# VectorE and SP zero stack rows, images and joined weights moved, sum of projections begun ahead, finer steps and a new merge table in a two-layer transformer kernel

## What is computed

```
h  = softmax over the batch of (cond . x) / sqrt(128), times x
x1 = x + bitlinear(silu(bitlinear(h, w_gate)) * bitlinear(h, w_up), w_down)
        # weights ternary, activations rounded to 8 bit per row; inner width 512
c  = causal attention, 16 heads of 8, over x1 plus one image key and value per head
        (k_img, v_img from cond), then c_proj
m  = attention, 16 heads of 8, no mask, over c (in_proj), then out_proj
x3 = layernorm(c + m) * g1 + b1
moe: router over 4 groups x 2 experts; out = weight * (relu(x3 W1 + b1) W2 + b2),
        8 experts of width 256, all computed for all rows
y  = x1 + layernorm(x3 + moe) * g2 + b2
```

## Time and profile before

| what | value |
| --- | --- |
| median of 3 runs | 382.31 us (380.33 to 384.16) |
| profiled execution, time | 381.2 us |
| profiled execution, span | 379.4 us |
| VectorE busy | 261.2 us (69%) |
| ScalarE busy | 171.2 us (45%) |
| GpSimd busy | 42.5 us (11%) |
| mean granted TensorE clock | 0.927 of full |

### The profile page before, as it was taken

How to read it: one execution, slowest core, us unless ns; L and a number is a source line. 1 busy time by engine, 2 the same in 40 slices (tenths; PEclk the granted TensorE clock), 3 DMA queues, 4 the chain that set the end, 5 groups by cost and what they waited for, 6 DMA issues and landing times.

```text
span 379.4 us, 5450 instructions
## 1 busy us (share of the span) xinstructions
PE 307.3 (81%) x1900; PEld 153.9 (41%) x1900; DVE 261.2 (69%) x763; ACT 171.2 (45%) x246; POOL 42.5 (11%) x56
## 2 busy tenths in 40 slices
PE   0251985897898999868999989999999987987980
PEld 0120733253453644433433222343434455655760
DVE  3979457997786887869989878877721135557444
ACT  2664134005455657443678565665777511220210
POOL 9189500000000000000000000002000001001001
PEclk9996566558999999999999999999999999999997
DMA  6101307601670004710006700160000000000001
GB/s 184 46 2 18 46 0 214 146 1 50 177 141 1 3 4 148 184 41 2 2 14 189 168 4 0 29 196 2 2 2 0 0 2 0 3 0 28 2 0 29
DMA packets 14719, 19.69 MB, mean 52 GB/s; under 512 B 2142, under 2 KB 12258, under 8 KB 14116
## 3 DMA queue, kind: packets, MB, share of 16 engines
q1 hardware_dynamic: 14404, 19.06, 19.3%
q0 software_dynamic: 288, 0.28, 0.6%
HBM read 13.99 MB, written 4.72 MB: 49 GB/s over the span
## 4 chain that ended last, share of the span: by engine, by line
PE 48%; DVE 24%; issue 14%; DMA 6%; ACT 5%; POOL 1%; SPq 1%; POOLq 0%; DVEq 0%; ACTq 0%
PE ps_pv L1273 11%; DVE mx L972 8%; PE ps_s L1232 8%; PE ps_t L1255 7%; DMA Qs<-nmT 5%; PE ps_s L1342 4%; PE ps_misc L1350 3%; PE ps_misc L1208 2%; DVE shared L968 1%; DVE shared L809 1%; DVE probs L902 1%; DMA X<-in_x 1%; ACT probs L751 1%; PE ps_misc L1238 1%; DVE mx L968 1%
## 5 line engine op out<-in xcount | busy, mean ns | idle before, releaser
L751 ACT ACTIVATE probs<-ps_t 128x1024 f32<-128x1024 f32 (+2 forms) x128 | 106.6, 862 | 62.9 <-PE ps_t L1258 33.9
L972 DVE TENSOR_REDUCE mx<-ps_s 128x1 f32<-128x512 f32 x128 | 82.0, 686 | 14.2 <-PE ps_s L1232 14.0
L1232 PE MATMUL ps_s<-Ks,Qs 128*128 128x512 bf16 (+3 forms) x237 | 78.0, 353 | 9.5 <-DVE mx L972 3.0
L1255 PE MATMUL ps_t<-Qs,Ks 128*128 128x512 bf16 (+3 forms) x256 | 67.9, 340 | 5.2 <-DMA Qs<-nmT 5.1
L1273 PE MATMUL ps_pv<-probs,Vs 128*32 128x512 f32 (+3 forms) x512 | 57.2, 524 | 0.4 <-ACT probs L751 0.2
L968 DVE CUSTOM_DVE_ANT_0 shared<-ps_s,shared 128x256 bf16<-128x256 f32 (+3 forms) x109 | 47.3, 465 | 10.9 <-PE ps_s L1232 10.3
L1232 PEld LDWEIGHTS ps_s<-Ks,Qs 128*128 128x128 bf16 x237 | 22.4, 99 | 65.5 <-DVE mx L972 30.8
L1074 DVE SCALAR_TENSOR_TENSOR shared<-ps_misc,comb,shared 128x128 f32<-128x128 f32 x64 | 18.1, 344 | 31.3 <-PE ps_misc L1350 31.1
L1350 PE MATMUL ps_misc<-Ks,shared 128*128 128x128 f32 x256 | 31.6, 277 | 5.5 <-DVE shared L1074 2.4
L1255 PEld LDWEIGHTS ps_t<-Qs,Ks 128*128 128x128 bf16 x256 | 23.5, 98 | 30.9 <-issue 8.0
L1350 PEld LDWEIGHTS ps_misc<-Ks,shared 128*128 128x128 f32 x256 | 30.5, 192 | 11.9 <-issue 11.5
(11 more groups left out here) (240 smaller groups left out, 361.9 us busy)
## 6 DMA issues: line engine op xcount, KB each, us to landing
parts_q<-Qp SPq DMA_DIRECT2D x20, 128.0 KB, 2.0
Qs<-parts_q SPq DMA_DIRECT2D x24, 96.0 KB
Ks<-parts_k SPq DMA_DIRECT2D x24, 96.0 KB
Qs<-parts_q SPq DMA_DIRECT2D x12, 192.0 KB
Ks<-parts_k SPq DMA_DIRECT2D x12, 192.0 KB
parts_k<-Kp SPq DMA_DIRECT2D x12, 128.0 KB, 1.8
Ks<-in_L_ffn_w SPq DMA_DIRECT2D x1, 1024.0 KB, 5.8
X<-in_x SPq DMA_DIRECT2D x2, 256.0 KB, 4.4
```

Source lines behind the costliest of these rows:

```text
L751: act.activation(probs[:, half % 2, j, 0:w], ps[:, 0:w], ACT.Exp).then_inc(free[f"t{i % 2}"], 1)
L972: last = dve.tensor_reduce(mx[:, b, t, h:h + 1], ps[:, 0:w], AX, ALU.max)
L1232: mm = pe.matmul(ps[:, 0:w], Qs[:, b, h, t * P:(t + 1) * P], Ks[:, b, h, 0:w], start=True, stop=True)
L1255: mm = pe.matmul(ps[:, col:col + w], Ks[:, b, h, kb * P:(kb + 1) * P], Qs[:, b, h, S - w:S], start=True, stop=(a >= 2))
```

## The change

- **Zeroing.** GpSimd no longer zeroes the upper stack rows. VectorE zeroes those of Qs, batch 0, as its first instruction; SP copies them to the three other stacks by DMA behind the loads of `setup`. A new step `fixed_rows` (SP) writes the constant rows and waits for these copies; so does the send of instances 0 and 1. The value stacks stay on GpSimd, each zeroed in four instructions.
- **Start.** Rounding of batch 1 is a step `round_x` of its own, behind `turn_down`. The image values and joined weights are a step `images` of their own. The residual of a batch is a step `x1` of its own (VectorE), apart from the transposes `x1t`.
- **Sum.** TensorE begins the sum in `presum` (one bias matmul over 512 columns, then the first projection) and ends it in `sum`. The sum of batch 1 lies in bank pv instead of misc. X3, the norm statistics and the router's transposed weights have a place for each batch.
- **Finer steps.** Engine parts that stood in one step have steps of their own: q_parts, k_parts, send, v_bias (VectorE, VectorE, SP, VectorE); image (TensorE); keep (ScalarE); normalise, centre, spread, routed, acc0, add (VectorE); relu (ScalarE and VectorE). centre has also the power on GpSimd, spread the second half of the norm. GpSimd's small loads are a step `load_small` that comes in the attention of instance 3.
- **Merge table.** The table is new, with 681 steps for 576. Spelled out, it begins: setup, ffn_in 0, turn_down, round_x, ffn_up 0.0, ffn_in 1, ffn_up 0.1 to 0.3, turn_weights, ffn_up 1.0, r2t and down 0.0 to 0.3, prepare, x1 0, ffn_up 1.1, images, ffn_up 1.2, x1t 0, ffn_up 1.3, q 0, k 0, q_parts 0, k_parts 0, r2t and down 1.0 to 1.3, x1 1, stacks 0, fixed_rows, send 0, stacks 1, scores 0.0 to 0.28, x1t 1, scores to 0.35, max 0.0, image 0.0, scores to 0.39, q 1, scores to 0.42, max_rows 0.0, scores to 0.45, k 1, scores to 0.48, v 0, q_parts 1, scores 0.49, attend 0.0. The old one has ffn_up 1.0 to 1.2 ahead of the first r2t, prepare with the images ahead of x1t 0, x1t 1 ahead of scores 0.0, then scores to 0.37, max 0.0, scores to 0.41, v 0, scores to 0.45, q 1, max_rows 0.0, scores to 0.47, k 1, scores to 0.49, attend 0.0. After the last values the new one goes: hidden 0.2, normalise, turn_back, hidden 0.3, o_rows, relu, presum 1, add, y 0.2, relu, sum 1, hidden 0.4, y 0.3, centre 1, hidden 0.5, add, relu, spread 1, y 0.4, add, hidden 0.6, x3t 1, y 0.5, hidden 0.7, router 1, ..., and ends hidden 1.7, y 1.6, add, centre, spread, out, y 1.7.

The diff, cut to its core:

```diff
+SUM_AT = ("misc", "pv")
 MERGE = (
-...
+    "ffwTfgfffwgffffffffwugUgfgff44ggggggggvSV4S00000000000000000000000000000g0000000mi0000g000m000g0"
+    "00f50A0AAE0A050Ag0AA500FAA00a00i000a1a1mM1aA1Am1A111a11A1A1A1A11aaI11AA1M1aa1A1A11a11IAA1a1A1A1A"
...
+    "C3m3lC3C3c33c3C3cD33cDK33cO3D3DcK3D3dSD33c3DD33n33QQnddDdPD3D3dLD33Dn3D3DmnDQmdQexddDdPDnDeDnDDd"
+    "QDLxddDDyzDLDPddDzDdDdDDyPxdddeLdedxszyxseyRezxRyzesyesxzxRRzyesxyzxesyRozexyoezxzyeyxezxyzexyey"
+    "zxzzpoppy"
...
+        "w": [("turn_down", 0, 0), ("turn_weights", 0, 0), ("prepare", 0, 0)],
+        "S": [("stacks", 0, 0), ("stacks", 1, 0), ("load_small", 0, 0)],
+        "T": [("round_x", 0, 0)],
+        "U": [("images", 0, 0)],
+        "V": [("fixed_rows", 0, 0)],
         "g": ffn(1) + qkv(1),
+        "u": [("x1", 0, 0)],
+        "v": [("x1", 1, 0)],
+        "i": both("image", 2),
         "m": [(n, a, g) for a in range(INST) for g in range(2) for n in ("max", "max_rows")],
         "q": qkv(2),
         "r": qkv(3),
         "l": [("load_experts", 0, 0)],
-        "n": route(0),
-        "s": route(1),
-        "e": each("hidden", 0, EXPERTS) + each("hidden", 1, EXPERTS),
-        "y": each("y", 0, EXPERTS) + each("y", 1, EXPERTS),
-        "o": [("out", 0, 0)],
-        "p": [("out", 1, 0)],
+        "e": both("hidden", EXPERTS),
+        "x": both("relu", EXPERTS),
+        "y": both("y", EXPERTS),
+        "z": both("add", EXPERTS),
     }
     for a in range(INST):
         chains["0123"[a]] = each("scores", a, HEADS * NT)
+        chains["4567"[a]] = [(n, a, 0) for n in ("q_parts", "k_parts", "send")]
+        chains["EFGH"[a]] = [("v_bias", a, 0)]
         chains["ABCD"[a]] = each("attend", a, UNITS)
         chains["abcd"[a]] = output(a)
+        chains["MNOP"[a]] = each("keep", a, ROUNDS)
+        chains["IJKL"[a]] = each("normalise", a, ROUNDS)
+    for b in range(B):
+        chains["ns"[b]] = [(n, b, 0) for n in ("presum", "sum", "x3t", "router", "combine", "bias2")]
+        chains["QR"[b]] = [(n, b, 0) for n in ("centre", "spread", "routed", "route", "acc0")]
+        chains["op"[b]] = [("centre", b, 1), ("spread", b, 1), ("out", b, 0)]
...
+                    sp.wait_ge(rows_first, 1)
+                    for stack in (Ks[HALF_ROWS:, 0, :, :], Qs[HALF_ROWS:, 1, :, :], Ks[HALF_ROWS:, 1, :, :]):
+                        sp.dma_start(stack, Qs[HALF_ROWS:, 0, :, :]).then_inc(rows_zeroed, 16)
+                if step == "fixed_rows":
                     sp.wait_ge(pool_const, 1)
                     sp.wait_ge(mparts_ready, 1)
+                    sp.wait_ge(rows_zeroed, 16 * 3)
...
-                if step == "v":
+                if step == "send":
                     if a >= 2:
                         sp.wait_ge(free["misc"], filled("misc", "o_rows", b))
                         sp.dma_start(Qs[SHIFT:MASK + PARTS, b, :, :],
                                      zrow[:, :].unsqueeze(1).to_broadcast([2 + PARTS, HEADS, S]))\
                           .then_inc(no_extra[a], 16)
+                    if a < 2:
+                        sp.wait_ge(rows_zeroed, 16 * 3)
...
-                    then_wait(pool.memset(Qs[HALF_ROWS:, 0, :, :].rearrange("p h s -> p (h s)").bitcast(fp32), 0.0))
-                    pool.memset(Ks[HALF_ROWS:, 0, :, :].rearrange("p h s -> p (h s)").bitcast(fp32), 0.0)\
-                        .then_inc(rows_zeroed[0], 1)
-                    pool.wait_ge(rows_zeroed[0], 1)
                 if step == "stacks":
-                    then_wait(pool.memset(Vs[:, 0, :, :, :], 0.0))
-                    pool.memset(Vs[:, 0, :, :, HD:HD + 1], 1.0).then_inc(stack_init[0], 1)
-                    pool.wait_ge(stack_init[0], 1)
-                    then_wait(pool.memset(Qs[HALF_ROWS:, 1, :, :].rearrange("p h s -> p (h s)").bitcast(fp32), 0.0))
-                    pool.memset(Ks[HALF_ROWS:, 1, :, :].rearrange("p h s -> p (h s)").bitcast(fp32), 0.0)\
-                        .then_inc(rows_zeroed[1], 1)
-                    pool.wait_ge(rows_zeroed[1], 1)
-                    then_wait(pool.memset(Vs[:, 1, :, :, :], 0.0))
-                    pool.memset(Vs[:, 1, :, :, HD:HD + 1], 1.0).then_inc(stack_init[1], 1)
+                    for t in range(NT):
+                        last = pool.memset(Vs[:, a, t, :, :], 0.0)
+                    then_wait(last)
+                    pool.memset(Vs[:, a, :, :, HD:HD + 1], 1.0).then_inc(stack_init[a], 1)
+                if step == "load_small":
                     for dst, src in (
...
-                if step in ("sum", "out"):
-                    norms += 1
-                    pool.wait_ge(ve_ready, norms)
-                    pool.tensor_tensor(rstd[:, :], ve[:, :], halves[:, :], ALU.pow).then_inc(rstd_ready, 1)
+                if step == "centre":
+                    n = 2 * i + a
+                    pool.wait_ge(ve_ready[n], 1)
+                    pool.tensor_tensor(rstd[:, n, :], ve[:, n, :], halves[:, :], ALU.pow).then_inc(rstd_ready[n], 1)
...
-                    ps = take("pv", "values", a, i // NT)
-                    act.activation(Ou[:, i // NT % 2, :], ps[:, :], ACT.Copy).then_inc(free["pv"], 1)
-                if step == "hidden":
+                if step == "keep":
+                    ps = take("pv", "values", a, i)
+                    act.activation(Ou[:, i % 2, :], ps[:, :], ACT.Copy).then_inc(free["pv"], 1)
+                if step == "relu":
                     ps = take("s1", "hidden", a, i)
...
+            def centre(n, src, dst, gain):
                 for t in range(NT):
-                    last = dve.bn_stats(stats[:, t, :], src[:, t, :])
+                    last = dve.bn_stats(stats[:, n, t, :], src[:, t, :])
                 then_wait(last)
                 for t in range(NT):
-                    last = dve.bn_aggr(mv[:, t, :], stats[:, t, :])
+                    last = dve.bn_aggr(mv[:, n, t, :], stats[:, n, t, :])
                 then_wait(last)
-                norms[0] += 1
-                dve.tensor_scalar(ve[:, :], mv[:, :, 1], EPS, None, ALU.add).then_inc(ve_ready, 1)
-            def norm(src, dst, gain, more, read_out, count):
+                dve.tensor_scalar(ve[:, n, :], mv[:, n, :, 1], EPS, None, ALU.add).then_inc(ve_ready[n], 1)
                 for t in range(NT):
-                    read = dve.scalar_tensor_tensor(out=dst[:, t, :], in0=src[:, t, :], scalar=mv[:, t, 0:1],
+                    read = dve.scalar_tensor_tensor(out=dst[:, t, :], in0=src[:, t, :], scalar=mv[:, n, t, 0:1],
                                                     in1=norm_gb[:, gain, :], op0=ALU.subtract, op1=ALU.mult)
-                read.then_inc(read_out, 1)
-                dve.wait_ge(read_out, count)
-                dve.wait_ge(rstd_ready, norms[0])
+                return read
+            def spread(n, dst, more):
+                dve.wait_ge(rstd_ready[n], 1)
                 for t in range(NT):
-                    last = dve.scalar_tensor_tensor(out=dst[:, t, :], in0=dst[:, t, :], scalar=rstd[:, t:t + 1],
+                    last = dve.scalar_tensor_tensor(out=dst[:, t, :], in0=dst[:, t, :], scalar=rstd[:, n, t:t + 1],
                                                     in1=more(t), op0=ALU.mult, op1=ALU.add)
                 return last
...
                 if step == "setup":
+                    dve.memset(Qs[HALF_ROWS:, 0, :, :].rearrange("p h s -> p (h s)").bitcast(fp32), 0.0)\
+                       .then_inc(rows_first, 1)
...
                     ternary(0)
+                    ternary(1)
                     rounded_x(0)
-                    ternary(1)
                     then_wait(dve.tensor_scalar(q1[:, 2, :], q1[:, 0, :], 1.0 / 127.0, None, ALU.mult))
                     dve.tensor_scalar(q1[:, 4, :], q1[:, 2, :], wmean[:, 1:2], None, ALU.mult)
                     dve.tensor_scalar(q1[:, 3, :], q1[:, 2, :], wmean[:, 0:1], None, ALU.mult).then_inc(scale_ready, 1)
+                if step == "round_x":
                     rounded_x(1)
...
+                if step == "centre" and i == 0:
                     dve.wait_ge(in_moe, 16 * 9)
-                    norm_stats(take("misc", "sum", a)[:, :].rearrange("p (t d) -> p t d", d=D))
-                    norm(place["misc"][:, :].rearrange("p (t d) -> p t d", d=D), X3[:, :, :], 0,
-                         lambda t: norm_gb[:, 1, :], free["misc"], filled("misc", "sum", a)).then_inc(x3_ready, 1)
-                if step == "router":
+                    ps = take(SUM_AT[a], "sum", a)[:, :].rearrange("p (t d) -> p t d", d=D)
+                    centre(a, ps, X3[:, a, :, :], 0).then_inc(free[SUM_AT[a]], 1)
...
+                if step == "presum":
+                    pe.wait_ge(bias_ready, 1)
+                    pe.wait_ge(free["misc"], filled("misc", "o_rows", a))
+                    ps = put(SUM_AT[a], "sum", a)
+                    pe.matmul(ps[:, :].rearrange("p (t d) -> p t d", d=D), ones[0:1, :],
```

(21 more changed lines are left out.)

119 lines of the change are left out of this document (61 added, 58 removed).

## The result

The changed kernel took **354.04 us** in the median of 4 runs (352.93 to 355.0), the kernel before 381.32 beside it (380.18 to 384.16): ratio 0.927, interval 0.921 to 0.934. That is 27.3 us less; I had forecast 15.2 less, 366 us, with a range down to 356. The sign was right and the size was not. The profiled execution took 352.93 us, its span 351.1 where the one before had 379.4.

The account below looks back on a forecast made before the run. TensorE, busy in 81% of the span, was taken as the bound from the first attention weights to the last values. Gains 7.5 + 1.5 + 0 + 0.8 + 5.4 = 15.2 us, from 381.2 us, gave 366 us, range 356 to 375.

Parts of the forecast that it names:

- Start, 7.5: Everything up to the first scores: 7.5 us faster, bounds 4 to 11.
- (a): Start: the four big memsets leave GpSimd, so VectorE's stalled L824 gives 1.25 us and L913 3.1 us.
- (e): Start: the old L919 stall, 1.3 us, goes; the Vs memsets left on GpSimd cost the new L919 0.9 (0 to 1.8).
- (f): Start: images and joined weights moved behind batch 0's residual and one up step; 1.3 us given back, x1t 6.7 earlier.
- rival 1: TensorE's clock comes back early, speeding images, q, k and the first scores: 5 to 7 us better, 360; chance 0.2.
- First scores, 1.5: First scores to first attend: VectorE's wait for q's first part goes, TensorE becomes the bound; 1.5 us faster, -1 to 2.7.
- Middle, 0 and 0.8: Attention to last values: order gives 0 us (minus 5 to plus 5), merging the first sum's four bias matmuls 0.8.
- Tail, 5.4: Last values to last y: fewer TensorE waits, second bias and layout give 5.4 us, bounds 2.5 to 7.
- The layout: Tail: new step order laid out, ending 62.9 us after the last values against 68.3.
- End, 0: Norm and store after TensorE's last matmul: the last 8.8 us are the same chain, no gain.

Follow-up runs that it names:

- first stage in the old order: Changed kernel with the steps from the first scores to attend step 3 in the order of the kernel before: ratio 0.945 to the kernel before.
- steps coupled in the tail: Changed kernel with the finer steps after the last values put back right behind their TensorE steps, last norm behind the last add: ratio 0.944 to the kernel before.
- the kernel with GpSimd's zeroing: Changed kernel with the stack rows zeroed by four GpSimd memsets again, all else kept: ratio 0.959 to the kernel before.
- the kernel with the rows sent first: Changed kernel with the last stack DMAs of instances 1 to 3 issued behind the maxima's rows of the instance before: ratio 0.917 to the kernel before, median 349.07 us.
- the kernel with the late Vs memsets: Changed kernel with GpSimd's Vs memsets held back until the last r2 of batch 1: ratio 0.933 to the kernel before.

## Why the prediction was wrong

**Start, 7.5, measured 10.4.** The stalls (a) went as priced, up steps (18.4 forecast, 18.16) and r2t (30.2, 29.61) too. The Vs stall (e) cost at most 0.3, not 0.9. The miss is at x1t, 10.2 us earlier where (f) gave 6.7: up to 2.3 of it is the images' rate. Starts with the same instructions put x1t at 40.0 to 40.4 in five profiles, in which the granted clock fell at 36 to 37 us, and at 42.5 to 42.7 in four: in three of these it had fallen by 25.0, 25.0 and 29.0, in the fourth the pairs took 0.79 us at full granted clock. The kernel before has both outcomes too: 50.55 with a fall at 30.5, and 48.1 with a fall at 46.0 and the rows sent first, whose start is the same. So this part of rival 1 came true in the profile, but by luck: with the same start the clock falls early or late, no cause is shown, and filling the hole with matmuls did not keep it.

**First scores, 1.5, measured 4.6: a step that failed.** I had the row, VectorE busy 21.0 of 22.5 us, called the engines nearly level and made TensorE the bound of the new order. The old order in the changed kernel gave back 4.3 us at an unchanged clock. I should have laid out VectorE's own work to the first attend, as I did for the tail: 23.9 us of work in 27.5 before, and 1.8 of it moved out. At a lower clock TensorE does count (24.4 to 24.7 us above), but even then the stage is 2.8 us shorter than before.

**Middle, 0 and 0.8, measured 5.7: the second step, and the larger miss.** I took the distance from max_rows to attend in TensorE's steps for the wait, and could not tell the sign from it. The waits are set by the stack packets ahead of the rows: sending the rows first shortened the stretch by 7.1 us in the old order, to 201.0, and by 3.9 in the new, to 198.7. So 2.3 us are the table's own, the bias matmul included (forecast 0.8; what the rest is, is not shown), and 3.2 are rows waits with what hangs on them (the 7.1 us are 2.0 more than the 5.1 of the earlier trace rows). The one profile with 6.3 us of waits and a clock fall, 207.9 us, is an outlier: in the ten others with the new zeroing and this table's steps there, the stack writes ahead of the rows, the stretch took 202.6 to 205.4.

**Tail, 5.4, measured 6.7.** Mechanism right: the bank frees y (3.9 us of waits when undone), the order of small steps 2.8, the sum begun ahead 1.0; they overlap. The layout ended at 62.9, the trace at 61.6.

**End, 0, measured 0.9.** VectorE's and GpSimd's chain is the same. The store is issued 2.7 us before the end of the span and was issued 3.6 before it. From the start of the last y group to the end the kernels with the old order have 9.1, 8.7, 8.2 and 8.1 us, and those with the new order between 8.1 and 9.1, so the 0.9 lies within what differs without the change.

The ratios 0.927 and 0.932 make 353.5 and 355.2 us of the 381.2 from which I forecast, and my range began at 356. So the result lies just outside, and the images' rate alone, up to 2.3 us, can move a run across the end. But the 15.2 itself was short, by 2.9 us in the start, 3.1 in the first scores, 4.9 in the middle, 1.3 in the tail and 0.9 at the end of the profiled execution.

## What to carry to other kernels

Before calling a stage level between two engines, add up the busy time of each in it and the work that the new order moves across its end. A small transfer that is waited for is late by what stands ahead of it on the DMA engines: look at which bulk transfers are issued before it and send what is needed later behind it; the price of the wait can be more than its length, since the clock may fall behind it. What is won in the start has to be read again at the end of the next stage: first scores 2.8 and 1.9 us earlier became 1.2 and nothing at the first attend.

## What the hardware showed that I had not expected

The price of a rows wait. Behind waits of 3.28 and 3.39 us TensorE's granted clock was 0.51 for 6.8 us, behind 2.64 (first stage in the old order) and 2.41 (steps coupled in the tail) for 3.4 us; behind the 2.55 above, and behind 3.05 in the kernel with GpSimd's zeroing, it stayed at 1.00. So the length of the wait alone does not decide it, and one profile of each kernel does not show that the wait is the reason: the kernel with the rows sent first has a fall of 3.4 us in its tail, at 313 us, with no wait for rows anywhere.

The granted clock is not all of TensorE's rate. In the kernel with the late Vs memsets the images' window has it in full, and yet their pairs take 0.79 us and not 0.48:

```profile
35.40:42.10 6.70, 6.70 (x20) 4.49 (x19) 3.74 (x14) 0.69 (x1) 0.00 (x0) 1.00 0.17 24
```

```profile
35.97 0.79 PE L1162 MATMUL ps_s<-brow,ones 1*128 1x128 f32 x2
```

What a matmul of a known shape takes is the safer reading in a start.
